# Causal attention: new weights for dealing out the maxima, and rows of maxima copied inside a step with a diagonal

## What is computed

```python
def _L3_attn_ref(x, Wq, bq, Wk, bk, Wv, bv, Wp, bp, rel_bias_table):
    N_HEADS = 16            # D = 8, T = 2048
    ...
    q = heads(x @ Wq + bq)
    k = heads(x @ Wk + bk)
    v = heads(x @ Wv + bv)
    ...
    q = q * cos + rotate_half(q) * sin
    k = k * cos + rotate_half(k) * sin
    ...
    att = jnp.einsum('bhid,bhjd->bhij', q, k) + bias[None]
    att = att * (1.0 / math.sqrt(D))
    causal = pos[None, :] <= pos[:, None]
    att = jnp.where(causal[None, None], att, -jnp.inf)
    att = jax.nn.softmax(att, axis=-1)
    y = jnp.einsum('bhij,bhjd->bhid', att, v)
    y = y.transpose(0, 2, 1, 3).reshape(B, T, C)
    return y @ Wp + bp
```

## Time and profile before

| | |
|---|---|
| median of 3 runs | 3386.45 us (3386.17 to 3389.59) |
| the profiled execution's own time | 3386.32 us |
| its span, from the first to the last instruction | 3384.5 us |
| granted TensorE clock, mean, as a share of 2.4 GHz | 0.936 |
| busy over the whole span: PE, DVE, ACT, POOL | 3007.2, 2441.6, 1803.6, 851.1 us |

### The profile page before, as it was taken

How to read it: one execution, slowest core, us unless ns; L and a number is a source line. 1 busy time by engine, 2 the same in 40 slices (tenths; PEclk the granted TensorE clock), 3 DMA queues, 4 the chain that set the end, 5 groups by cost and what they waited for, 6 DMA issues and landing times. The chain is left out here.

```text
span 3384.5 us, 61888 instructions
## 1 busy us (share of the span) xinstructions
PE 3007.2 (89%) x24429; PEld 1635.3 (48%) x24469; DVE 2441.6 (72%) x5485; ACT 1803.6 (53%) x3298; POOL 851.1 (25%) x809
## 2 busy tenths in 40 slices
PE   4878579898799999998899879798998899998999
PEld 3435456566323333333566557476776222333677
DVE  8898678777599999994877853735336888884433
ACT  2223347777478777776777743133222466777211
POOL 0334147766100000001966710101303111212000
PEclk8899889999799999999999989898999689899899
DMA  1065221111320000000211110001102300000100
GB/s 54 9 156 141 68 63 33 37 31 25 119 112 1 2 1 1 2 1 26 65 25 37 29 34 1 2 28 63 44 1 69 112 32 1 35 2 1 48 1 13
DMA packets 77879, 129.20 MB, mean 38 GB/s; under 512 B 12772, under 2 KB 52616, under 8 KB 77384
## 3 DMA queue, kind: packets, MB, share of 16 engines
q1 hardware_dynamic: 77592, 125.25, 13.0%
HBM read 77.39 MB, written 34.19 MB: 33 GB/s over the span
## 5 line engine op out<-in xcount | busy, mean ns | idle before, releaser
L2065 ACT ACTIVATE AR<-ps 128x1024 f32<-128x1024 f32 (+2 forms) x756 | 717.9, 996 | 247.6 <-PE ps L1966 182.1
L2152 DVE TENSOR_REDUCE AR<-ps 128x1 f32<-128x512 f32 x1296 | 809.1, 683 | 38.3 <-PE ps L1935 37.4
L1966 PE MATMUL ps<-AR 32*128 32x512 bf16 (+3 forms) x4992 | 524.2, 379 | 5.4 <-ACT AR L2065 3.8
L1935 PE MATMUL ps<-AR 32*128 32x512 bf16 (+3 forms) x1664 | 484.3, 399 | 40.2 <-DVE AR L2152 14.1
L1983 PE MATMUL ps<-AR 128*32 128x512 f32 (+3 forms) x3328 | 438.2, 600 | 9.2 <-ACT AR L2070 6.7
L2562 PEld LDWEIGHTS ps<-AR 128*128 128x128 f32 x3072 | 363.2, 192 | 60.3 <-issue 47.4
L2721 DVE SCALAR_TENSOR_TENSOR X<-ps,AR,X 128x128 f32<-128x128 f32 x512 | 143.7, 344 | 342.9 <-PE ps L2562 342.5
L1935 PEld LDWEIGHTS ps<-AR 32*128 32x128 bf16 x1664 | 121.0, 93 | 524.9 <-DVE AR L2152 392.9
L2562 PE MATMUL ps<-AR 128*128 128x128 f32 x3072 | 363.3, 276 | 0.0
L2537 PE MATMUL ps<-XT,AR 128*128 128x512 f32 x672 | 307.8, 594 | 0.1
L206 POOL TENSOR_TENSOR rs<-rs,halves 128x4 f32<-128x4 f32 x48 | 49.5, 1031 | 831.6 <-DVE rs L198 831.6
(11 more groups left out here) (326 smaller groups left out, 5010.1 us busy)
## 6 DMA issues: line engine op xcount, KB each, us to landing
AR<-AR SPq DMA_DIRECT2D x124, 128.0 KB, 2.3
band<-AR SPq DMA_DIRECT2D x32, 450.0 KB, 5.1
AR<-band SPq DMA_DIRECT2D x32, 448.0 KB, 5.2
AR<-in_c_rot SPq DMA_DIRECT2D x64, 128.0 KB, 2.3
AR<-in_L3f_w SPq DMA_DIRECT2D x30, 256.0 KB, 6.0
rows_KA<-AR SPq DMA_DIRECT2D x32, 128.0 KB, 2.4
AR<-scr_bias SPq DMA_DIRECT2D x32, 128.0 KB, 3.2
AR<-in_L2f_w SPq DMA_DIRECT2D x30, 128.0 KB, 2.7
```

What stands on the lines that cost most here:

```text
L1935: e.matmul(g.bank[b][:, 0:w], QA[rows, q, 128 * i:128 * i + 128], KA[rows, q, 512 * first:512 * first + w], start=way != "kept", stop=True ...
L1966: t = e.matmul(g.bank[self.base[i, u] + h % 2][:, lo:512], K[32 * h:32 * h + 32, q, 128 * kt:128 * kt + 128], Q[32 * h:32 * h + 32, q, que ...
L2065: e.activation(dst[:, :, lo:512], src[:, :, lo:512], ACT.Exp, scale=self.scale).then_inc(*s.up("exp" if u else "left", k, i, *((1,) if u e ...
L2152: e.tensor_reduce(o, g.bank[b][:, 0:w], AXX, ALU.max).then_inc(*s.up("reduced", k, n, h, st, kc))
```

## The change

It has two parts. First, the weights `area` of the causal stage are replaced. They were 0.15 + 0.85 x (share of the 512 queries computed) + 0.35 if the step is near: 1.0 for a far step and 1.35, 1.35, 1.14, 0.93, 0.71 for the five kinds of near steps in their order. `free_time` gives 1.0 to a far step, 0.67 to a near step with 256 near queries and 0.46 to one with 128 (the first and the last kind). Through `begin` they also set `rate` and `lead`. Second, where the rows of maxima are turned in a near step, ACT's copy is taken out of its place behind the step (`early` remembers the step) and put between the two halves of that step: after the near copy and the exponential right of it, before the wait for the bias of the second pair. The copy itself is the same; `copy_rows` holds it.

```diff
--- before.py
+++ after.py
@@ -1558,6 +1558,11 @@
         a, z = max(128 * kt, 512 * qc), min(128 * kt + 256, 512 * qc + 512)
         return (a, z) if self.causal and z > a else None
 
+    def free_time(self, n, kt):
+
+        near = self.near_cols(n, kt)
+        return 1.0 if not near else 0.67 if near[1] - near[0] == 256 else 0.46
+
     def hold(self, b, *closers):
 
         old, self.left[b] = self.left[b], closers
@@ -1590,7 +1595,7 @@
         self.plan.append(("max", n, st, kc, out))
 
     def plan_rows_max(self, n):
-        b = self.spare()
+        b = self.rows_bank[n] = self.spare()
         self.plan.append(("max_rows", n, b, self.hold(b, ("max_row", n))))
 
     def plan_finish(self, n):
@@ -1626,12 +1631,13 @@
         causal, rounds, last_kt = self.causal, self.rounds, self.last_kt
         self.plan, self.left, self.rows_made = [], {b: () for b in range(8)}, set()
         self.base, self.free_from, pairs_used = {}, None, 0
+        self.early, self.rows_bank = {}, {}
         self.ring = self.closed = 0
         self.banks, self.slot = (5, 6, 7), {}
         self.steps = steps = [(n, kt) for n in range(16) for kt in range(last_kt[n] + 1)]
         area = [(512 - self.low(n, kt)) / 512.0 for n, kt in steps]
         if causal:
-            area = [0.15 + 0.85 * x + (0.35 if self.near_cols(n, kt) else 0.0) for (n, kt), x in zip(steps, area)]
+            area = [self.free_time(n, kt) for n, kt in steps]
         self.begin, at = {}, 0.0
         for (n, kt), a in zip(steps, area):
             self.begin.setdefault(n, at)
@@ -1726,6 +1732,8 @@
                 if pk == last_kt[pn]:
                     finish_due.append(pn)
             if self.rows_due:
+                if self.near_cols(n, kt):
+                    self.early[i] = self.rows_due[0]
                 self.plan_rows_max(self.rows_due.pop(0))
             for x in slots[3]:
                 self.plan_max(*x)
@@ -2036,12 +2044,8 @@
                             e.wait_ge(*s.at("reduced", k, *in_kept[y]))
                         in_kept[y] = n, h, st, kc + 1
                         e.activation(self.KEPT[:, y, :], g.bank[b], ACT.Relu).then_inc(*s.up("kept", k, n, h, st, kc))
-            if what == "max_rows":
-                n, b, _ = x
-                gr, qc = self.rounds[n]
-                e.wait_ge(*s.at("m_turned", k, n))
-                e.activation(self.rows["QC"][:, gr % self.slots, chunk(qc)], g.bank[b], ACT.Copy).then_inc(
-                    *s.up("max_row", k, n))
+            if what == "max_rows" and x[0] not in self.early.values():
+                self.copy_rows(e, s, x[0])
             if what == "step":
                 i, n, kt = x
                 near, lo = self.near_cols(n, kt), self.low(n, kt)
@@ -2058,6 +2062,8 @@
                             e.activation(dst[:, :, end:512], src[:, :, end:512], ACT.Exp, scale=self.scale).then_inc(
                                 *s.up("left", k, i))
                         continue
+                    if u and i in self.early:
+                        self.copy_rows(e, s, self.early[i])
                     if u and near:
                         e.wait_ge(*s.at("biased", k, i))
                     else:
@@ -2079,6 +2085,13 @@
         for c in range(4):
             e.wait_ge(*s.at("turned", k, c, "out"))
             e.activation(g.XT[:, chunk(c)], g.bank[c % 2], ACT.Copy).then_inc(*s.up("xt", k, c, "out"))
+
+    def copy_rows(self, e, s, n):
+
+        gr, qc = self.rounds[n]
+        e.wait_ge(*s.at("m_turned", self.k, n))
+        e.activation(self.rows["QC"][:, gr % self.slots, chunk(qc)], self.g.bank[self.rows_bank[n]], ACT.Copy).then_inc(
+            *s.up("max_row", self.k, n))
 
     def last_step(self, n):
         return sum(z + 1 for z in self.last_kt[0:n + 1]) - 1
```

## The result

The kernel after takes 3418.97 us (median of 4 runs, 3417.06 to 3425.07), the one before 3388.02 us beside it: a ratio of 1.0094, with a 95% interval from 1.0076 to 1.0111. That is 31 us, or 0.9%, slower. The forecast was 7.6 us slower, and 3418.97 lies above its range.

The account below looks back on a forecast made before the run. No engine was full in the long part of causal attention; a step cost the larger of its two loads, or more. Terms 4.9 + 0.5 - 5 + 7.2 = +7.6 us gave 3394.0 us, range 3377 to 3408.

Parts of the forecast that it names:

- the loads: Causal loop, steps 4 to 139: the new weights' shift of maxima from near to far steps costs +4.9 us.
- the sum: Causal loop: each step's larger of floor and DVE's work, added up; 385.7 us before, 390.6 after.
- the predicted +7.2: Nine early copies in near steps: ACT waits for turned maxima, 0.8 us each, +7.2 us, range 4.5 to 12.6.
- The -5 us for the bank stall: Causal loop: PE no longer waits for the bank held by late copies, -5 us, between bounds 4.2 and 7.4.
- the second cost: Loop time above the summed loads, 25 us before; its change taken as +0.5 us, bounds -3 and +15.
- faster: Rival: lighter near blocks let steps average and may keep 2.4 GHz; about 3375.7 us, chance 0.20.
- the upper bound in the prediction: Far stretches: +15 us, at 1.4 us per added far step with eight or more maxima.
- An empty step repays nothing: Causal loop: a step costs the larger of its two loads, or more; DVE's surplus isn't averaged over neighbours.
- the floors: Per step, what PE and ACT need with DVE idle: 2.36 us for a far step without maxima.

Follow-up runs that it names:

- e1: The kernel after with every copy of the rows of maxima at its old late place, new weights kept: 3407.09 us, ratio 1.0057.
- e7: The kernel after with the early copy moved behind the whole second exponential, ahead of the near one's: 3404.63 us, ratio 1.0046.
- e8: The kernel after, unchanged, run and profiled once more: 3417.09 us, ratio 1.0079 against the kernel before.
- e10: The kernel after (copy early) with each reduction of the causal stage reading only 128 columns: 3329.20 us, ratio 0.9826.
- e9: e1 (copy late) with each reduction of the causal stage reading only 128 columns: 3321.46 us, ratio 0.9801.
- e2: The kernel after with the old weights put back, early copy kept: 3387.49 us, ratio 1.000.
- e12: e1 with 272 matmuls for maxima issued twice into the same bank, in steps with more than three units: 3420.73 us, ratio 1.01.
- e3: e1 with the new weights multiplied by 1.288, so they add up to the old sum: 3393.29 us, ratio 1.0014.
- e4: e1 with the old weights multiplied by 0.7764, so they add up to the new sum: 3386.99 us, ratio 0.9993.
- e5: The kernel before with two neighbouring far steps' maxima given to the first, none to the second: 3424.30 us, ratio 1.0105.
- run 17: Not a run label: a verb and a time, in "these run 17 to 35 us of the block at 1.2 GHz".
- e6: The kernel before with weights searched for the smallest sum of the larger of DVE's work and floor: 3390.25 us, ratio 1.0006.
- e11: The kernel after with the old weights times 0.7764 and the copy placed as in e7: 3380.80 us, ratio 0.9979.

## Why the prediction was right and wrong

**The direction was right, and the loads came out, in part by luck.** With 0.28 us taken off for each us at 1.2 GHz, e1's loop is 424.9 - 30.5 = 394.4 us and that of before 410.7 - 21.3 = 389.4. The difference is 5.0, and the predicted term was +4.9. That they meet within 0.1 is luck: e7, with the same loads, gives 3.2. The last maxima stand in step 137 before and 138 after (the prediction says 138 both times), and the 44 us behind the loop became 45.5. Steps 40 to 50 got 15.6 us longer where 9 to 11 was said. The near blocks that were said to lose 2 to 4 us went from 21.3 to 18.1 (steps 7 to 11), 19.1 to 14.3 (19 to 23), 16.4 to 15.6 (35 to 39), 17.5 to 13.6 (99 to 103) and 14.9 to 13.8 (115 to 119); steps 51 to 55 got longer, 13.7 to 15.3. Four of the ten near blocks lie within 2 to 4. All near blocks together won 20.5 us where the sum said 27.6.

**The early copy: the loss was right, the gain did not come.** Near blocks of the kernel after are together 7.2 us longer than those of e1. That they meet the predicted +7.2 so exactly is luck too: 1.9 of it goes with 6.9 us more at 1.2 GHz, and the second execution (e8), with the clock of e1, gives 5.8. e10 against e9 gives 7.7 by its medians. So the price is 5.3 to 7.7 us, inside the stated 4.5 to 12.6. The timeline of ACT in the kernel after, step 35 (round 4's copy, a near step without maxima), with PE's and DVE's rows between them:

```profile
2787.14 0.39 ACT L2059 ACTIVATE AR<-ps 128x256 f32<-128x256 f32 x1 [0.92 <-PE ps L1974]
2787.43 0.81 ACT L2062 ACTIVATE AR<-ps 128x768 f32<-128x768 f32 x1
...
2788.55 0.38 PE L1958 MATMUL ps<-identb,AR 128*128 128x128 bf16 x4
2788.97 0.60 ACT L2093 ACTIVATE AR<-ps 128x512 bf16<-128x512 f32 x1 [0.74 <-PE ps L1958]
2789.46 1.02 ACT L2071 ACTIVATE AR<-ps 128x1024 f32<-128x1024 f32 x1
2790.37 0.42 ACT L2076 ACTIVATE AR<-AR 128x256 f32<-128x256 f32 x1
...
2790.68 0.60 ACT L2059 ACTIVATE AR<-ps 128x512 f32<-128x512 f32 x1
```

The same step in e1, copy late, ACT alone:

```profile
2784.17 0.38 ACT L2057 ACTIVATE AR<-ps 128x256 f32<-128x256 f32 x1 [0.92 <-PE ps L1972]
2784.45 0.81 ACT L2060 ACTIVATE AR<-ps 128x768 f32<-128x768 f32 x1
2785.14 1.03 ACT L2069 ACTIVATE AR<-ps 128x1024 f32<-128x1024 f32 x1
2786.04 0.43 ACT L2074 ACTIVATE AR<-AR 128x256 f32<-128x256 f32 x1
2786.35 0.61 ACT L2091 ACTIVATE AR<-ps 128x512 bf16<-128x512 f32 x1
2786.83 0.62 ACT L2057 ACTIVATE AR<-ps 128x512 f32<-128x512 f32 x1
```

From the first piece of this step to the first piece of the next are 3.54 us (2790.68 - 2787.14) with the copy early and 2.66 (2786.83 - 2784.17) with it late. ACT was ready at 2788.23 and stood 0.74 us for the turning, which in PE's queue has the values of the step before in front of it. They end at 2788.11, and in this step GpSimd's split of the maxima ends 0.08 us later still, at 2788.19. In seven of the nine early copies in the loop PE goes from the values to the turning without a pause. The idle time is 0.74 of the 0.88. The estimate per copy was 0.8. The Trainium skill (Perfetto Trace Analysis, Per-engine timelines) calls ScalarE strict FIFO. The trace agrees: the exponential of 2789.46 had its scores long before and was not pulled ahead.

The -5 us for the bank stall were foretold whichever part of the change would bring them. The wait of PE's loads for the copies did fall, from 7.4 us to 5.0 in e1, to 2.8 after and to 2.6 in e2, and that of its matmuls from 4.2 to 1.7, 1.2 and 0.8. But no loop shows a gain: e1 has its +5.0 with this gain inside, and e2's loop at the full clock is 389.6 against 389.4. Two readings are left, and no run separates them. Either a stall that is taken away from PE where DVE or ACT ends last is worth nothing, or another cost of its size (in e2 that of the early copy) stands in its place.

**The step that failed.** It is the term for the second cost, which the prediction took as +0.5 us out of bounds from -3 to +15, with this argument: "Steps 24 to 34 have a crowded step and nothing above their sum, so the cost doesn't simply go by crowded steps; I stay near the low end". The cost is TensorE's clock, and the argument mistook a stretch at 2.4 GHz for the general case. The loop's account, after minus before:

- loads, by the sum over steps: 4.9 (e1 at the full clock: 5.0)
- copy: +6.7, the loop of after less that of e1, both at the full clock, where +7.2 was said; and 0 for the freed bank where -5 was said
- clock: 0.28 x (104.9 - 75.1) = +8.4, where +0.5 was said

Together 20.0, as measured. The copy's and the clock's terms are taken from the loops themselves, so the only test in this agreement is that of the loads. Of the 23 us by which the forecast missed, the clock is 8 and the freed bank 5. Outside the loop come 1.5 + 1.2 in the same stage and the 8 us of unchanged stages, for which the prediction had no term. The prediction knew the clock but looked at one side alone: as a gain, in near blocks that become lighter. That may have come (58 us at 1.2 GHz became 28, but e2 has 33 with the old plan). What it did not ask is what the crowded *far* steps do to it, and there 17 us (36 in e2) became 77. The timeline of the kernel after in steps 13 and 14 shows one:

```profile
2716.58 2.48 DVE L2165 TENSOR_REDUCE AR<-ps 128x1 f32<-128x512 f32 x4 [0.43 <-PE ps L1943]
...
2717.86 1.94 PE L1991 MATMUL ps<-AR 128*32 128x512 f32 x8
...
2720.37 2.48 DVE L2165 TENSOR_REDUCE AR<-ps 128x1 f32<-128x512 f32 x4 [1.30 <-PE ps L1943]
...
2721.66 1.02 ACT L2071 ACTIVATE AR<-ps 128x1024 f32<-128x1024 f32 x1 [3.52 <-PE ps L1974]
...
2722.93 1.94 PE L1991 MATMUL ps<-AR 128*32 128x512 f32 x8
```

From these values to the next (steps 13 to 14) the kernel after and e12, which has the same reductions, have the windows

```profile
2717.86:2722.93 5.07, 5.07 (x26) 1.17 (x26) 3.69 (x7) 1.30 (x2) 0.00 (x0) 0.50 0.01 3
2725.07:2728.42 3.35, 3.22 (x28) 0.95 (x27) 2.92 (x6) 1.20 (x2) 0.00 (x0) 1.00 0.00 0
```

The values take 1.94 us here against 1.07 at 2.4 GHz, and the stretch 5.07 us against 3.35 in e12. ACT stands 3.52 us for scores. DVE, for whose sake PE had waited, now itself stands 1.30 us for the next maximum, since the matmul for it comes behind the slow values. By the profile, where PE's times are modelled, PE is busy all of the 5.07 us and DVE 3.69: what the stretch waits for is now PE. So crowding costs twice, once by DVE's surplus and once by the slow PE that it leaves behind.

What did PE do before the clock fell? In the kernel after it fell to 1.2 GHz at 2712.0. From 2708.7 on six of PE's loads had stood for reductions, 0.27 to 0.51 us each; two of them:

```profile
2709.91 0.09 PEld L1943 LDWEIGHTS ps<-AR 32*128 32x128 bf16 x1 [0.34 <-DVE AR L2165]
2710.51 0.09 PEld L1943 LDWEIGHTS ps<-AR 32*128 32x128 bf16 x1 [0.51 <-DVE AR L2165]
```

Such waits alone are not the sign of it. In this block PE's loads stood 12.6 us for reductions in e1 (clock 0.57), but also 12.6 in the kernel before (0.96) and 13.2 in e12 (1.00); in e9 it is 7.2. What differs by the edits of e9 and e12 is how much of the block's time PE has work: e9 shortens the time, e12 adds work. That this is what the clock follows is inferred from these two. The Trainium skill (TensorE: Matmul & The Clock Gate, A second HAM failure mode) describes the clock swinging with short waits between groups of matmuls while PSUM banks are cycled. The clock of steps 12 to 18, 0.60 here and 1.00 in e9, agrees with it; that of the kernel before, 0.96 with as long waits as e1, does not. The prediction had cited the page for the near blocks, where it spoke for *faster*.

What does tell the plans apart in this block is DVE's load as a whole. Steps 12 to 18 in e3, e4 and e5:

```profile
2700.43:2735.67 35.24, 34.46 (x183) 8.12 (x182) 24.88 (x50) 13.88 (x15) 0.00 (x0) 0.50 0.00 1
2704.61:2727.68 23.07, 22.57 (x177) 6.99 (x176) 20.19 (x44) 14.37 (x17) 0.33 (x1) 0.83 0.00 1
2701.52:2726.14 24.62, 22.39 (x178) 6.38 (x177) 20.61 (x45) 13.81 (x16) 0.63 (x1) 0.93 0.00 1
```

By the planner's formula DVE has 25.6 us of work there in after, e8, e1, e7 and e3, and these run 17 to 35 us of the block at 1.2 GHz. It has 20.7 in before, e2, e4, e5, e6 and e11, and these run 2 to 8. e5 belongs to the second group although its steps hold up to 12 maxima: the low clock goes with the load of the block, not with how it is dealt to the steps.

**A crowded far step as a unit.** By my sums the loop lay above its sum by 25.0 us in the kernel before (11 crowded far steps), 22.9 in e4 (12), 36.4 in e3 (21) and 34.3 in e1 (22): some 11 us and 1.1 for each crowded far step. So the upper bound in the prediction, 1.4 each, was near the truth for these four plans. (Its 15 us for far stretches are 16.8 by the same cuts: 219.9 measured, 203.1 by the sum.) It fails for e5 and e6: e5 has by far the most crowded steps and lies only 3.8 us above its sum (438.1 and 434.3), e6 41.6 above. So this unit is a mixture, not a law. Taking 0.28 us off for each us at 1.2 GHz does better: the loops of before, e1, e2, e3, e4, e7 and e11 then lie 1.3 to 6.1 us above their sums. It too fails for e6 (11.8 above) and for e5 (28 below), so it holds only for plans made like these.

**Do steps average?** "An empty step repays nothing" was too strong. e5's block of 28.30 us refutes it for far steps that alternate at 2.4 GHz. The witness for it, steps 24 to 34 at 28.16 us against a sum of 28.3, was misread: e9 takes 28.02 us for the same steps, with more maxima in them and DVE busy for only 13.33, and in the kernel before PE is busy for 27.46 of the 28.16 us. So this block was close to PE's own time, which the floors had left out, and it met DVE's sum by accident. What could not be averaged is a whole stretch beyond its floor: in steps 40 to 50 DVE has 38.0 us to do over floors of 26.0, and they took 45.39. The +4.9 came out near enough nevertheless, probably because much of the moved work went into such stretches; no run shows that by itself.

**Open.** Why the clock stayed low in steps 40 to 50 of e12, with PE busy for 48.55 of 50.42 us by the profile. How much of the 8 us in unchanged stages is scatter: the part ahead of the stage differed by 4.0 us between the two profiled executions of the same kernel (first values at 2647.6 and 2643.5), and it was longest but for e12 in e4 (2648.1), whose median equals that of the kernel before. Over both rounds the eight executions of the kernel after took 3405.61 to 3425.07 us. No run isolates it. What sets the clock exactly: e9 and e12 move it, but no run changes PE's waits and nothing else.

## What to carry to other kernels

When work is moved from one stretch to another, ask of *both* what becomes of PE's waits and of its clock, and price a stretch at 1.2 GHz with rows at 1.2 GHz; a block that met its sum at 2.4 GHz is no witness for one that will be crowded. Weights of a planner do two things, they share out and they set the pace, and each was nearly harmless here while both together cost 18.5 us: change them one at a time. A copy that waits for another engine belongs behind one piece of independent work on its own queue; one exponential of 1.02 us between was enough here. And read the floor of a step with the work in it that is to be moved there, on every engine that takes part in it: steps without maxima hid 2 us of PE's own time in steps 24 to 34.

## What the runs showed of the hardware

- The granted clock differs between executions of one program in the same block: in steps 12 to 18 of the kernel after, 27.2 us of 34.0 at 1.2 GHz in one and 16.9 of 30.5 in the other. One us at 1.2 GHz went with 0.28 us of time in this stage, by the fit over its blocks.
- More matmuls made a block shorter: steps 12 to 18 took 33.18 us with 183 records of PE at a clock of 0.57, and 25.81 us with 214 at 1.00.
- With 168 us less work on DVE (348.8 to 181.2) the loop got 76 us shorter (424.9 to 348.9), of which an estimated 0.28 x 93 = 26 us are the clock's.
